# Attention scores as pairs of half-height matmuls, and a new order of TensorE's and VectorE's work

## The reference

```python
h = patches @ W.T + b + pos                               # (32, 1024, 64)
q, k, v = h @ Wq.T + bq, h @ Wk.T + bk, h @ Wv.T + bv
scores = where(mask, q @ k.T / 8, -1e9)                   # 1024 x 1024 an image
a = where(mask, softmax(scores), 0) @ v @ Wo.T + bo
h = layernorm(h + a)
probs = softmax(h @ gate_w + gate_b); e = argmax(probs)
y = relu(h @ w1[e] + b1[e]) @ w2[e] + b2[e]               # for the tokens within the capacity
out = layernorm(h + nan_to_num(y * probs[e] * kept))
```

## Time and profile before

| | |
|---|---|
| runs without a profile | 1121.2 us median of 3 (1120.86 to 1123.85) |
| profiled execution | span 1163.1 us, mean granted TensorE clock 0.939; no other time of it is given |
| busy share of the span | TensorE 89%, VectorE 78%, ScalarE 63%, GpSimd 60% |
| chain that ended last | TensorE 55%, VectorE 24%, issue 10%, ScalarE 4% |
| steps 0 to 30 | from 37.8 to 973.1 us of the span |
| copies in SBUF of q and k | six of 256 KB an image |

### The profile page before, as it was taken

How to read it: one execution, slowest core, us unless ns; L and a number is a source line. 1 busy time by engine, 2 the same in 40 slices (tenths; PEclk the granted TensorE clock), 3 DMA queues, 4 the chain that set the end, 5 groups by cost and what they waited for, 6 DMA issues and landing times.

```text
span 1163.1 us, 18855 instructions
## 1 busy us (share of the span) xinstructions
PE 1029.4 (89%) x5534; PEld 582.2 (50%) x5534; DVE 902.7 (78%) x1847; ACT 728.6 (63%) x1142; POOL 692.6 (60%) x689
## 2 busy tenths in 40 slices
PE   4899999999999999999999999999999999736640
PEld 2455555555555555555555555555555555423320
DVE  5557787789898988889888988898988887654542
ACT  2255455667777777677777776776777667535540
POOL 0014445447676676667767666766666767765665
PEclk8699999999999999999999999999999999866775
DMA  5324335444444443535344443443453613034300
GB/s 129 93 69 106 96 89 141 111 104 111 115 122 115 109 121 96 148 87 150 95 125 120 114 104 106 124 119 101 106 137 79 154 37 92 20 96 121 98 18 10
DMA packets 76732, 118.93 MB, mean 102 GB/s; under 512 B 16652, under 2 KB 52959, under 8 KB 76630
## 3 DMA queue, kind: packets, MB, share of 16 engines
q1 hardware_dynamic: 59798, 100.61, 34.6%
q0 software_dynamic: 16832, 17.11, 4.6%
HBM read 49.64 MB, written 18.11 MB: 58 GB/s over the span
## 4 chain that ended last, share of the span: by engine, by line
PE 55%; DVE 24%; issue 10%; ACT 4%; SPq 2%; another core or an unknown queue 1%; POOL 1%; DMA 1%; POOLq 0%; DVEq 0%; ACTq 0%
PE p_u L575 15%; DVE mx L979 8%; PE p_st L559 8%; PE p_st L562 7%; PE p_sm L545 5%; PE p_misc L508 4%; PE p_misc L531 4%; PE p_misc L638 3%; PE p_misc L654 2%; PE p_misc L590 2%; ACT xh L754 2%; DVE ld L1045 1%; POOL out L1355 1%; DVE tt L1006 1%
## 5 line engine op out<-in xcount | busy, mean ns | idle before, releaser
L1343 POOL DMA_INDIRECT slots<-rows,idx x256 | 261.7, 1022 | 220.5 <-issue 151.4
L771 ACT ACTIVATE pT<-p_st 128x1024 f32<-128x1024 f32 x256 | 262.2, 1024 | 171.9 <-PE p_st L562 131.4
L979 DVE TENSOR_REDUCE mx<-p_sm 128x1 f32<-128x1024 f32 x252 | 307.3, 1220 | 80.1 <-PE p_sm L545 69.5
L1355 POOL DMA_INDIRECT out<-b_o,b_ix x270 | 286.9, 1063 | 111.9 <-issue 73.4
L575 PE MATMUL p_u<-pT,vv 128*64 128x512 f32 x1024 | 263.8, 615 | 0.0
L559 PE MATMUL p_st<-mQ,sK 128*128 128x512 f32 x512 | 184.2, 441 | 5.5 <-ACT pT L771 3.6
L562 PE MATMUL p_st<-mR,sR 72*128 72x512 f32 x512 | 161.8, 397 | 0.0
L545 PE MATMUL p_sm<-sK,mQ 64*128 64x512 f32 x252 | 130.7, 519 | 6.9 <-DVE mx L979 3.4
L559 PEld LDWEIGHTS p_st<-mQ,sK 128*128 128x128 f32 x512 | 79.7, 190 | 104.5 <-issue 81.3
L545 PE MATMUL p_sm<-hi,mQ 64*128 64x512 f32 x252 | 130.6, 518 | 0.0
L562 PEld LDWEIGHTS p_st<-mR,sR 72*128 72x128 f32 x512 | 97.4, 190 | 22.9
(11 more groups left out here) (194 smaller groups left out, 1550.4 us busy)
## 6 DMA issues: line engine op xcount, KB each, us to landing
b_w<-in_w SPq DMA_DIRECT2D x136, 193.5 KB
mQ<-hi SPq DMA_DIRECT2D x64, 256.0 KB
b_in<-slots SPq DMA_DIRECT2D x136, 66.0 KB
sK<-hi SPq DMA_DIRECT2D x32, 256.0 KB
sK<-lo SPq DMA_DIRECT2D x32, 256.0 KB
mR<-lo SPq DMA_DIRECT2D x32, 256.0 KB
sR<-hi SPq DMA_DIRECT2D x32, 256.0 KB
xt<-in_x SPq DMA_DIRECT2D x32, 196.0 KB
```

Of the source, the lines that this page charges most:

```text
L771: act.activation(pT[k % 4][:, :], flat(p_st), ACT.Exp).then_inc(exp_done, 1)
L979: dve.tensor_reduce(mx[:, p, j:j + 1], flat(max_place(n, j)), AX.X, ALU.max).then_inc(max_done, 1)
L1343: pool.indirect_dma_start(slots, bass.IndirectOffsetOnAxis(ap=idx[:, p, j:j + 1], axis=0), rows[:, p, j, :], None, bounds_check=SLOTS - 1, ...
L1355: pool.indirect_dma_start(out_rows, bass.IndirectOffsetOnAxis(ap=b_ix[:, o, j:j + 1], axis=0), b_o[:, o, j, :], None, bounds_check=T - 1, ...
```

## The change

Scores of a tile become eight matmuls of 64 rows in four pairs, one of a pair on partitions 0 to 63 for queries 0 to 511, its partner on 64 to 127 for the others: three products and, as the fourth pair, ones times the shift `sh` (128 x 512). They need q and k parts on both halves of the partitions: `hx` and `lx` are `hi` and `lo` with their halves swapped, and SyncE makes them by four copies (one of them half as long). `mQ`, `sK`, `mR` and `sR` are gone; `hi`, `lo`, `hx` and `lx` have three buffers each. The maxima are turned with 128 stationary columns. `max_scores` stands right behind `scores`; the first weighted sum of an image is whole; `up` stands behind the row-max pair, and `down` as well, so beside the last weighted sum of the step. On VectorE `row_max` comes first at each j, then `qk_low` at j = 0 and `attend` at j = 1; what reads `p_sm` is a function of its own (`slot_read`), right behind `shift`; the table functions come one j earlier (`full_units` and `past_experts` together); `split_low` moves from j = 0 to the end of the step. SyncE loads `xr` last in its step. The cut diff:

```diff
+QT = HALF // P
-        c_neg = sb("c_neg", [E, E])
+        c_neg = sb("c_neg", [P, QT])
-        hi = [sb(f"hi{i}", [P, S], F32R) for i in range(2)]
-        lo = [sb(f"lo{i}", [P, S], F32R) for i in range(2)]
-        mQ = [sb(f"mQ{i}", [P, S], F32R) for i in range(3)]
-        sK = [sb(f"sK{i}", [P, S], F32R) for i in range(3)]
-        mR = [sb(f"mR{i}", [P, S], F32R) for i in range(2)]
-        sR = [sb(f"sR{i}", [P, S], F32R) for i in range(2)]
-        mx = sb("mx", [P, 2, NT])
+        hi = [sb(f"hi{i}", [P, S], F32R) for i in range(3)]
+        lo = [sb(f"lo{i}", [P, S], F32R) for i in range(3)]
+        hx = [sb(f"hx{i}", [P, S], F32R) for i in range(3)]
+        lx = [sb(f"lx{i}", [P, S], F32R) for i in range(3)]
+        sh = [sb(f"sh{i}", [P, HALF], F32R) for i in range(2)]
+        ones_r = sb("ones_r", [P, P], F32R)
+        mx = sb("mx", [P, 2, P])
...
-                par, tri = c % 2, (c + 2) % 3
+                par = c % 2
-                    made, used = sp.lower_val(b + 3), sp.lower_val(NT * b)
-                    sp.wait_ge(hi_ready, made)
-                    if has(-1):
-                        sp.wait_ge(st_done, used)
-                    for dst, src in ((mQ[tri][0:D, :], hi[par][0:D, :]), (mQ[tri][D:P, :], hi[par][0:D, :]),
-                                     (sK[tri][0:D, :], hi[par][D:P, :])):
-                        sp.dma_start(dst.bitcast(F32), src.bitcast(F32)).then_inc(spread_qk[tri], 16)
-                    sp.wait_ge(lo_ready, made)
-                    sp.dma_start(sK[tri][D:P, :].bitcast(F32), lo[par][D:P, :].bitcast(F32))\
-                        .then_inc(spread_qk[tri], 16)
+                    n, t = b + 2, (b + 2) % 3
+                    sp.wait_ge(hi_ready, n + 1)
+                    if n >= 3:
+                        sp.wait_ge(st_done, NT * (n - 2))
+                    for dst, src in ((hx[t][0:D, :], hi[t][D:P, :]), (hx[t][D:P, :], hi[t][0:D, :])):
+                        sp.dma_start(dst.bitcast(F32), src.bitcast(F32)).then_inc(spread_hi[t], 16)
+                    sp.wait_ge(lo_ready, n + 1)
+                    for dst, src in ((lx[t][0:D, :], lo[t][D:P, :]), (lx[t][D:P, HALF:S], lo[t][0:D, HALF:S])):
+                        sp.dma_start(dst.bitcast(F32), src.bitcast(F32)).then_inc(spread_lo[t], 16)
+                if chunk_of(b + 1) is not None:
+                    load_chunk(chunk_of(b + 1))
+                if has(3) and has(0):
+                    load_patches(b + 3, 1 - par)
+                if has(3) and has(1) and not has(0):
+                    load_patches(b + 3, 1 - par)
-                if chunk_of(b + 1) is not None:
-                    load_chunk(chunk_of(b + 1))
-                if has(3) and has(0):
-                    load_patches(b + 3, 1 - par)
-                if has(2):
-                    if has(0):
-                        sp.wait_ge(st_done, NT * b + NT)
-                    for dst, src in ((mR[par][0:D, :], lo[par][0:D, :]), (sR[par][0:D, :], hi[par][D:P, :])):
-                        sp.dma_start(dst.bitcast(F32), src.bitcast(F32)).then_inc(spread_r[par], 16)
-                if has(3) and has(1) and not has(0):
-                    load_patches(b + 3, 1 - par)
...
@@ -532,36 +528,39 @@
                                      xt[0:KTOK, p, t * P:(t + 1) * P], w_px[:, :], start=True, stop=True)
                 last.then_inc(v_done, 1)
 
-            def max_scores(n, t, nth, j):
+            def max_scores(n, j):
+                t = n % 3
                 if j == 0:
-                    pe.wait_ge(spread_qk[t], 64 * nth + 64)
+                    pe.wait_ge(spread_hi[t], 32 * (n // 3) + 32)
                     after(pe, shift_ready, n)
                     after(pe, pos_read, n - 2)
 
-                after(pe, max_done, j - 1 if isinstance(n, int) and n == 0 else NT * n + j)
-
-                for a, keys in ((0, sK[t]), (1, hi[n % 2])):
-                    h = slice(a * D, (a + 1) * D)
-                    last = pe.matmul(max_place(n, j)[:, a, :], mQ[t][h, j * P:(j + 1) * P],
-                                     keys[h, a * HALF:(a + 1) * HALF], start=True, stop=True)
-                last.then_inc(sm_done, 1)
+                after(pe, max_done, j - 1 if n == 0 else NT * n + j)
+
+                pe.matmul(max_place(n, j)[:, 0, :], hi[t][0:D, j * P:(j + 1) * P], hx[t][0:D, 0:HALF],
+                          start=True, stop=True)
+                pe.matmul(max_place(n, j)[:, 1, :], hx[t][D:P, j * P:(j + 1) * P], hi[t][D:P, HALF:S],
+                          start=True, stop=True).then_inc(sm_done, 1)
 
             def max_turn(n, p):
                 wait_apart(pe, max_done, NT * n + NT)
-                pe.transpose(p_sm[0:NT, 0, 0:P], mx[:, p, :], c_id[:, :]).then_inc(mt_done, 1)
-
-            def scores(n, p, t, k):
+                pe.transpose(p_sm[:, 0, 0:P], mx[:, p, :], c_id[:, :]).then_inc(mt_done, 1)
+
+            def scores(n, k):
+                t = n % 3
                 if k == 0:
-                    pe.wait_ge(spread_r[p], of_parity(n, p, 32))
+                    pe.wait_ge(spread_lo[t], 32 * (n // 3) + 32)
                     pe.wait_ge(shift_ready, n + 1)
                 after(pe, exp_done, NT * n + k)
-                for a in range(2):
-                    pe.matmul(p_st[:, a, :], sK[t][:, k * P:(k + 1) * P],
-                              mQ[t][:, a * HALF:(a + 1) * HALF], start=True, stop=False)
-                for a in range(2):
-                    last = pe.matmul(p_st[:, a, :], sR[p][0:D + NT, k * P:(k + 1) * P],
-                                     mR[p][0:D + NT, a * HALF:(a + 1) * HALF], start=False, stop=True)
-                last.then_inc(st_done, 1)
+                kt = slice(k * P, (k + 1) * P)
+                for upper, lower in ((hi, hx), (lo, lx)):
+                    pe.matmul(p_st[:, 0, :], hx[t][0:D, kt], upper[t][0:D, 0:HALF], start=upper is hi, stop=False)
+                    pe.matmul(p_st[:, 1, :], hi[t][D:P, kt], lower[t][D:P, HALF:S], start=upper is hi, stop=False)
+                pe.matmul(p_st[:, 0, :], lx[t][0:D, kt], hi[t][0:D, 0:HALF], start=False, stop=False)
+                pe.matmul(p_st[:, 1, :], lo[t][D:P, kt], hx[t][D:P, HALF:S], start=False, stop=False)
+                pe.matmul(p_st[:, 0, :], ones_r[0:D, :], sh[n % 2][0:D, :], start=False, stop=True)
+                pe.matmul(p_st[:, 1, :], ones_r[D:P, :], sh[n % 2][D:P, :], start=False, stop=True)\
+                    .then_inc(st_done, 1)
 
             def weighted_sum(n, p, r, halves=(0, 1)):
 
@@ -683,33 +682,31 @@
                     project(0, q, 0, True)
                 if has(2):
                     qk_product(b + 2, par)
+                m, back = chunk_of(b), chunk_of(b - 1)
                 for k in range(NT):
                     if has(0):
-                        scores(b, par, c % 3, k)
+                        scores(b, k)
+                    if has(1):
+                        max_scores(b + 1, k)
                     if has(-1):
                         if k == 0:
                             weighted_sum(b - 1, q, 3)
                         if k == 1:
                             turn_sums(b - 1, has(2))
                     if k == 2 and has(0):
-                        weighted_sum(b, par, 0, (0,))
-                    m, back = chunk_of(b), chunk_of(b - 1)
+                        weighted_sum(b, par, 0)
                     if m is not None and k == 2:
                         rows_turn(m)
                     if back is not None and b <= NB and k == 2:
                         pe.wait_ge(t_ready, min(b, NB))
                         turn_back(back)
+                    if has(1) and (k == 6 or k == 3 and b >= 0):
+                        project(b + 1, q, k // 6, has(2))
                     if m is not None and k in (4, 5):
                         up(m, k - 4)
                     if m is not None and k == 7:
                         down(m)
-                    if has(1):
-                        max_scores(b + 1, (c + 1) % 3, third(1), k)
-                        if k == 6 or k == 3 and b >= 0:
-                            project(b + 1, q, k // 6, has(2))
                     if has(0):
-                        if k == 2:
-                            weighted_sum(b, par, 0, (1,))
                         if k in (4, 5):
                             weighted_sum(b, par, 1, (k - 4,))
                         if k == 7:
...
@@ -964,28 +960,28 @@
                 dve.tensor_tensor(xl[D:KTOK, :], xr[D:KTOK, :], xh[D:KTOK, :].bitcast(F32), ALU.subtract)\
                     .then_inc(xl_ready, 1)
 
-            def qk_low(n, p, t, nth):
+            def qk_low(n):
                 dve.wait_ge(hi_ready, n + 1)
-                if not isinstance(n, int) or n >= 2:
-                    dve.wait_ge(spread_qk[t], 64 * nth + 64)
-                    dve.wait_ge(spread_r[p], of_parity(n - 2, p, 32))
```

(13 more changed lines are left out.)

63 lines of the change are left out of this document (30 added, 33 removed).

## The result

The changed kernel takes 1119.2 us (median of 9, 1118.7 to 1121.4) against 1123.9 for the kernel before (median of 9, 1120.9 to 1125.3): ratio 0.9968, 95% interval 0.9955 to 0.9981. The forecast was 1088, range 1070 to 1110: a gain, but 4.6 us by the medians in place of 33, and outside the range.

The account below looks back on a forecast made before the run. TensorE was taken to set the step, busy 30.5 of 30.8 us, VectorE next. Terms -25 - 5 + 2.5 - 5 = -32.5 from 1121.2 gave about 1088 us, range 1070 to 1110.

Parts of the forecast that it names:

- Pairs at 0.235: TensorE's scores: each half-height pair takes 0.235 us, so a tile stays at 0.94 us, no change.
- 18 entries for 24: TensorE, step with a chunk: fewer changes of matmul form, saving 1.1 us, less 0.10 for an exposed load.
- C: Rival on TensorE's scores: chained pairs run at 0.215 us like L638's, -20 us, 1068 us; chance 8%.
- D: Rival on TensorE's scores: weight loads of pairs are exposed, 3.3 us a step, 102 in all, 1190 us; chance 8%.
- E: Rival on TensorE: form entries don't vanish, as the chip drains for another reason; no change, 1121 us; chance 3%.
- The order: TensorE's merged forms: -1.0 us in 25 chunk steps (-25), and -5 us over six steps without a chunk.
- `xl` "is what is late next if VectorE slips": Step start: TensorE's L508 waits for `xl`, now late in VectorE's step, at 0.5 us; no cost was counted.
- VectorE's sum in table steps: VectorE needs 30.0 us against TensorE's 29.8, so +0.2 us in 13 table steps, +2.5 us.
- The forecast's own sign of being wrong: TensorE idling for reductions or `xl` by more than 0.5 us a step would show rival B.
- rival B: VectorE becomes the bound: 1115 us if it costs 0.8 us every step, 1098 in table steps alone; chance 20%.
- attend's stall: A longer weighted sum ahead of L606 covers its wait for `attend`: up to -10 us, half counted, -5.
- Queues: SyncE issues four copies for six and loads xr later, in time for ScalarE: cost 0.

Follow-up runs that it names:

- p: The changed kernel's half-height pairs, with the kernel before's order of TensorE's, VectorE's and SyncE's work: 1123.9 us, 0.9996 of the kernel before.
- e9: variant X with the table's first six operations before b_p, `centre` behind the gate's choice, GpSimd's rows operations behind its eighth transfer: 1094.0 us, 0.9738 of before.
- e1 again: variant X run a second time, on a chip without stalls: 1109.1 us, 0.9869 of the kernel before.
- variant X: The changed kernel with `xl` moved to row maximum 1: 1210.7 us (1.0354 of before) on a chip with stalls, 1109.1 us (0.9869) without.
- e6: variant X with `centre` behind the gate's choice and the table's operations one j later: 0.9943 of before among stalls, 1101.1 us (0.9798) without.
- e13: variant X with GpSimd's rows operations moved behind its last transfer of a chunk: 1265.9 us, 1.0926 of the kernel before, among stalls.
- e10: e9 with `centre` left ahead of the last row maximum: 1093.8 us, 0.9731 of the kernel before.
- e12: e10 with `xl` left last in VectorE's step: 1266.7 us, 1.0895 of the kernel before, among stalls.

## Why the prediction was wrong

- *Pairs at 0.235, entering 0.10, leaving 0.09, 18 entries for 24.* Right. The trace shows 0.23 to 0.24 a pair, and p shows that pairs alone cost nothing. Rivals C, D and E are out. (In D, 4 x 0.10 x 8 is 3.2 and not 3.3; its 1190 should be 1187.)
- *The order is worth 1.0 us a step, 30 us in all.* Right as a price for TensorE: e9, with the changed kernel's matmuls, is 30.7 us under before and 1.0 us a step under p. But it is the time that TensorE could give, and the changed kernel got 4.6 of it.
- *`xl` "is what is late next if VectorE slips", cost 0.* **The step that failed.** I had VectorE's idle times and didn't lay `xl` behind the last reduction on a clock: reduction to 525.97, gate's choice, `xl` to 527.65, where TensorE wanted it at 526.90. That needs no slip at all: step 2, which has no chunk, shows the same wait of 0.68 at 88.39. Moved to row maximum 1 it is worth 10.6 us. The forecast's own sign of being wrong was there: TensorE idled for `xl` and reductions 15.6 + 5.3 us between 65 and 950 us, 0.7 us a step and not under 0.5.
- *VectorE's sum in table steps, 29.7 - 0.5 + 0.7 + 0.1 = 30.0: "+2.5".* Undersized. The 0.71 is there, but two instructions are held beside GpSimd, 1.1 us each, where before only `ld` was (its 1.51 in the earlier trace rows was read, and put under rival B as a sign of tightness, not asked about). Held time between 200 and 950 us: 22 us before, 32 in p, 42 in the changed kernel, 0.7 in e9. The reordering shifted VectorE against GpSimd; that part of the loss is 15 us (e1 again to e9), together with the idle 1.0 us ahead of b_p that the table's operations now fill. Held time by itself doesn't give the loss: variant X has 45 us of it and e6 17, with table steps of 31.0 us in both. How much is due to the holds and how much to that idle 1.0 us isn't shown; e13, made to tell them apart, ran only among stalls.
- *attend's stall, -5.* Wrong: that stall shows only on the other kind of chip. In the result's trace it doesn't exist, and nothing was there to cover. A profile that is 42 us over the median of the runs was a warning not to price anything `remote` from it.
- *Queues, 0; exponentials, 0; setup, 0.* Right: TensorE waits 0.5 us in all on `p_st` between 65 and 950 us, and never for a copy there.
- *Rival B, VectorE the bound.* Nearest to what happened: TensorE waited for VectorE in nearly every step, as in its dearer case, which took 25 us off a gain of 31. Measured are 26.6 us (the changed kernel to e9, fourth batch). The 28 us by which the forecast was off are about these, less the 2.5 that its sum had, plus attend's 5. But in plain steps it wasn't VectorE's load, 26.2 us busy of 30.3; it was `xl`'s place in the queue.

On the chips without stalls e9 and e10 beat the kernel before by 2.6 and 2.7% and the changed kernel by 2.2 and 2.3%. They haven't run on the other kind, and e12, close to e10, took 1.09 there. e6 is under the kernel before on both kinds (0.980 and 0.994).

## What to carry to other kernels

When the engine at the bound gets faster, lay what its neighbours do in the last microseconds of a step on a clock, instruction by instruction; "cost 0, unless the other engine slips" isn't an answer when that engine is 28 us busy of 30. An instruction of eight elements a partition that takes 1.3 us is the most useful row in a timeline: look at what the other engines do at its end. And repeat a variant on a chip like the reference's before believing it: the same kernel was 0.987 of before on one chip and 1.035 on another.
